# In the last stretch of a macaron block, ACT and PE take over POOL's share of the routed sum

## What is computed

```python
x = x + 0.5 * ffn(layernorm(x))       # first feed-forward
x = x + attn(layernorm(x))
x = x + 0.5 * ffn(layernorm(x))       # second feed-forward, the same weights

# ffn(h): probs = softmax(h @ gate_W.T); the two largest are the gates
routed = sum over the 2 chosen e:  gate_e * (silu(h @ w1_e) * (h @ w3_e)) @ w2_e
shared = sum over the 8 shared n:  (silu(h @ w1_s) * (h @ w3_s)) @ w2_s / 8
ffn = 0.5 * shared + 0.5 * routed
```

## Time and profile before

| | |
|---|---|
| median of 3 executions | 809.51 us (806.77 to 810.10) |
| the profiled execution | 809.17 us |
| its span, first to last instruction | 807.4 us |
| PE busy in the span | 701.7 us (87%) |
| DVE busy | 456.2 us (57%) |
| ACT busy | 347.4 us (43%) |
| POOL busy | 445.1 us (55%) |
| last routed result on its way to DRAM | 765.3 us |
| the 16 loads of YF issued | 768.15 to 780.98 us |
| mean granted TensorE clock | 0.952 of full speed |

### The profile page before, as it was taken

One profiled execution on the slowest core, in us unless ns is written; L12 is line 12 of the kernel. 1 busy time (PEld: TensorE's weight loads), 2 busy tenths in 40 slices (PEclk: granted clock), 3 DMA queues, 4 the chain that ended last, 5 costly groups with the idle time before them and its releaser, 6 DMA issues. The chain is left out here.

```text
span 807.4 us, 12924 instructions
## 1 busy us (share of the span) xinstructions
PE 701.7 (87%) x4308; PEld 596.7 (74%) x4308; DVE 456.2 (57%) x1100; ACT 347.4 (43%) x889; POOL 445.1 (55%) x511
## 2 busy tenths in 40 slices
PE   3878987999999999957876699874999999999966
PEld 3766765888888888825654487663888888888855
DVE  7598672434444444359999828763444444443375
ACT  3612642444444444477764262551444444444410
POOL 6792017566766673479886250006566667664460
PEclk9979997999999999979999989996999999999988
DMA  9700002111111120221101000001111111111182
GB/s 310 273 1 1 1 4 54 37 46 49 48 46 48 47 49 28 72 72 53 41 13 40 27 27 1 1 2 42 37 48 47 47 50 47 48 46 32 37 241 72
DMA packets 45150, 44.03 MB, mean 55 GB/s; under 512 B 6048, under 2 KB 39840, under 8 KB 44704
## 3 DMA queue, kind: packets, MB, share of 16 engines
q1 hardware_dynamic: 35872, 24.32, 9.8%
q0 software_dynamic: 9216, 18.89, 8.3%
HBM read 27.46 MB, written 15.73 MB: 53 GB/s over the span
## 5 line engine op out<-in xcount | busy, mean ns | idle before, releaser
L598 POOL DMA_INDIRECT rows<-tokens,source x144 | 139.0, 965 | 160.2 <-issue 95.9
L613 POOL DMA_INDIRECT results<-yout,target x144 | 141.7, 984 | 112.9 <-DVE yout L937 76.2
L731 DVE TENSOR_TENSOR hr<-silu,psU 128x512 f32<-128x512 f32 x144 | 99.2, 689 | 180.7 <-PE psU L1229 179.4
L1149 ACT ACTIVATE silu<-psG 128x512 f32<-128x512 f32 x144 | 86.2, 598 | 186.4 <-PE psG L1229 186.2
L1379 PE MATMUL psY<-W,hT 128*128 x1120 | 147.9, 275 | 0.0
L1379 PEld LDWEIGHTS psY<-W,hT 128*128 128x128 f32 x1120 | 136.1, 192 | 0.0
L1142 ACT ACTIVATE hT<-psH 128x512 f32<-128x512 f32 x144 | 86.0, 597 | 78.2 <-PE psH L1362 78.2
L1362 PE MATMUL psH<-ident,hr 128*128 128x128 f32 x576 | 86.5, 272 | 0.0
L1362 PEld LDWEIGHTS psH<-ident,hr 128*128 128x128 f32 x576 | 71.9, 140 | 19.0 <-issue 0.2
L1227 PE MATMUL psG<-W13H,xTH 128*128 x144 | 69.6, 484 | 3.0 <-DVE xTL L913 3.0
L1100 ACT ACTIVATE silu<-psG 128x512 f32<-128x512 f32 x64 | 37.6, 591 | 79.4 <-PE psG L1229 54.9
(11 more groups left out here) (175 smaller groups left out, 1288.5 us busy)
## 6 DMA issues: line engine op xcount, KB each, us to landing
W<-w_e SPq DMA_DIRECT2D x3, 2048.0 KB, 14.2
tokens<-XN SPq DMA_DIRECT2D x16, 256.0 KB, 2.9
Y<-results SPq DMA_DIRECT2D x32, 128.0 KB, 2.3
YF<-results SPq DMA_DIRECT2D x16, 256.0 KB, 4.9
rows<-tokens,source POOLq DMA_INDIRECT x144, 2.5
results<-yout,target POOLq DMA_INDIRECT x144, 2.3
X<-x SPq DMA_DIRECT2D x8, 256.0 KB, 5.4
out<-X SPq DMA_DIRECT2D x8, 256.0 KB, 2.5
```

What stands on the lines that cost most here:

```text
L598: pool.indirect_dma_start(rows[:, g % RING, t, :], None, tokens, bass.IndirectOffsetOnAxis(ap=source[:, tile:tile + 1], axis=0))\
L613: pool.indirect_dma_start(results, bass.IndirectOffsetOnAxis(ap=target[:, tile:tile + 1], axis=0), yout[:, g % 2, t, :], None).then_inc(y_ ...
L731: dve.tensor_tensor(hidden, silu[:, s.u % 2, :], psU[:, s.u % 2, :], ALU.mult).then_inc(h_done, 1)
L1149: act.activation(silu[:, s.u % 2, :], psG[:, s.u % 2, :], ACT.Silu).then_inc(silu_done, 1)
```

## The change

POOL no longer adds anything in the tail. Chunks 0, 2 and 4, now `PE_CHUNKS`, are done by three engines. ACT scales each half of such a chunk by its gates in place, four copies of 128x128 behind silu(25) to silu(30): chunk 0 at k = 25 and 26, chunk 2 at 27 and 28, chunk 4 at 29 and 30. PE adds the two halves of a chunk in PSUM, two fp32 matmuls of 512 columns with the identity into a bank of `last_y`, behind in_shared(28), in_shared(30) and at k = 32, ahead of out_shared(28). DVE adds the bank to X, one instruction a chunk, one step later (k = 29, 31 and 33). DVE's own five chunks stay as they are, and so does their order. SP waits for the new semaphore for chunks 0, 2 and 4.

```diff
-POOL_CHUNKS = (0, 2, 4)
-DVE_CHUNKS = tuple(c for c in range(CHUNKS) if c not in POOL_CHUNKS)
+PE_CHUNKS = (0, 2, 4)
+DVE_CHUNKS = tuple(c for c in range(CHUNKS) if c not in PE_CHUNKS)
 HALF_STEP = 24
+SCALE_STEP = 25
+SUM_STEP = {28: 0, 30: 1, 32: 2}
+SUM_LAG = 1
...
 # POOL
-            link = Chain(pool, last_link_pool)
-            pool.wait_ge(sh_added, CHUNKS + FRONT[1])
-            for c in POOL_CHUNKS:
-                pool.wait_ge(yf_in[c], 16 * TOPK)
-                chunk = slice(c * CH, (c + 1) * CH)
-                ys, xs = YF[:, :, chunk, :], X[:, chunk, :]
-                link.then(pool.tensor_tensor(ys, ys, gates[:, :, chunk].unsqueeze(3).to_broadcast([P, TOPK, CH, D]),
-                                             ALU.mult))
-                link.then(pool.tensor_tensor(xs, xs, ys[:, 0, :, :], ALU.add))
-                pool.tensor_tensor(xs, xs, ys[:, 1, :, :], ALU.add).then_inc(last_added_pool, 1)
...
 # DVE
+                    def add_sums(n):
+                        dve.wait_ge(last_summed, n + 1)
+                        chunk = slice(PE_CHUNKS[n] * CH, (PE_CHUNKS[n] + 1) * CH)
+                        xs = X[:, chunk, :].rearrange("p t d -> p (t d)")
+                        dve.tensor_tensor(xs, xs, last_y[n % 2][:, :], ALU.add).then_inc(last_added_sums, 1)
+
                     for k in range(front[1], SHARED):
                         gated_shared(Step.of(k, 2 * FT))
                         if k % FT == 6 % FT and k // FT > FRONT[1]:
                             add_shared(k // FT - 1)
                         if k >= HALF_STEP:
                             add_half()
+                        if k - SUM_LAG in SUM_STEP:
+                            add_sums(SUM_STEP[k - SUM_LAG])
                     add_half()
+                    for k in range(SHARED, SHARED + 2):
+                        if k - SUM_LAG in SUM_STEP:
+                            add_sums(SUM_STEP[k - SUM_LAG])
                     dve.wait_ge(last_link, len(DVE_CHUNKS))
                     add_shared(CHUNKS - 1)
                     add_half()
...
 # ACT
                 for k in range(front[l], SHARED):
                     silu_shared(k)
+                    if l == 1 and k >= SCALE_STEP:
+                        n, half = divmod(k - SCALE_STEP, TOPK)
+                        if n < len(PE_CHUNKS):
+                            act.wait_ge(yf_in[PE_CHUNKS[n]], 16 * TOPK)
+                            for t in range(PE_CHUNKS[n] * CH, (PE_CHUNKS[n] + 1) * CH):
+                                i = act.activation(YF[:, half, t, :], YF[:, half, t, :], ACT.Copy,
+                                                   scale=gates[:, half, t:t + 1])
+                            i.then_inc(last_scaled, 1)
...
 # PE
+                def sum_results(n):
+
+                    pe.wait_ge(last_scaled, TOPK * (n + 1))
+                    if n == 0:
+                        pe.wait_ge(y_done, 2 * GROUPS)
+                    if n >= 2:
+                        pe.wait_ge(last_added_sums, n - 1)
+                    chunk = slice(PE_CHUNKS[n] * CH, (PE_CHUNKS[n] + 1) * CH)
+                    for k in range(TOPK):
+                        i = pe.matmul(last_y[n % 2][:, :], ident[:, :],
+                                      YF[:, k, chunk, :].rearrange("p t d -> p (t d)"),
+                                      start=(k == 0), stop=(k == TOPK - 1))
+                    i.then_inc(last_summed, 1)
+
                 for k in range(front[l], SHARED + 2):
                     if k < SHARED:
                         in_shared(Step.of(k, 2 * FT))
                     if k >= front[l] + 5:
                         out_shared(Step.of(k - 5, 2 * FT))
+                    if l == 1 and k in SUM_STEP:
+                        sum_results(SUM_STEP[k])
```

More of the change, by code:

```diff
@@ L392, in macaron @@
         last_link = sem("last_link")
-        last_link_pool = sem("last_link_pool")
         last_added = sem("last_added")
-        last_added_pool = sem("last_added_pool")
+        last_scaled = sem("last_scaled")
+        last_summed = sem("last_summed")
+        last_added_sums = sem("last_added_sums")
         routed_added = sem("routed_added")
@@ L486, in _ @@
                             sp.dma_start(YF[:, k, chunk, :], results_v[:, k, chunk, :]).then_inc(yf_in[c], 16)
-                    by_pool, by_dve = 0, 0
+                    by_pe, by_dve = 0, 0
                     for c in range(CHUNKS):
-                        if c in POOL_CHUNKS:
-                            by_pool += 1
-                            sp.wait_ge(last_added_pool, by_pool)
+                        if c in PE_CHUNKS:
+                            by_pe += 1
+                            sp.wait_ge(last_added_sums, by_pe)
                         else:
```

## The result

The changed kernel takes 802.51 us in the median of 5 runs (801.18 to 803.00), the kernel before 809.51 (806.77 to 810.33, five runs): a ratio of 0.9918, 95% interval 0.9899 to 0.9938. The profiled execution took 803.0 us with a span of 801.1. The prediction was 802.8 us.

The account below looks back on a forecast made before the run. The prediction took PE, waiting for DVE that POOL slows, as what holds up the tail. Waits and low clock of 11.5 us go, 5.2 of sums and 0.1 of wait come: 809.17 - 6.4 = 802.8 us, range 800.4 to 805.6.

Parts of the forecast that it names:

- the schedule: PE and DVE carried through the tail: PE bounds it from 774.8 to 796.3, what remains starts 6.4 us earlier.
- The cause: POOL, not the loads, slows DVE's `add_half` in the tail; without it two halves take 7.1 us less.
- The slower rival: In the tail the loads, not POOL, slow DVE and sums come on top: +4.5 to 5, some 814 us; chance 0.04.
- The sums: On PE in the tail, two fp32 matmuls of 512 columns take 1.73 us a sum, 5.2 us for three.
- out(c): The shared expert's second product on PE in the tail: 3.78 us, 3.84 in the last one.
- ACT: Scaling in the tail takes 1.17 us per four copies, mostly idle time; the rival that it comes late: 804.2 us, chance 0.05.
- PE as the bound: With POOL silent, PE bounds the tail from 774.8 to 796.3, with one gap of 0.1 us.
- The rival of the cheap sums: Tail sums at 0.93 us end PE 2.4 us earlier, h(31) late by up to 1.6: some 801 us; chance 0.05.
- The output transfers: SP's queue at the end of the tail: cost taken as 0, bound 0.5 us.
- The low clock as a term: PE's half speed in the tail costs 2.4 us and goes; the rival that it still falls: 805.2 us, chance 0.09.
- The cross-check: On PE between 774.76 and 802.7, 11.5 us of waits and low clock go, 5.2 of sums and 0.1 of wait come.

Follow-up runs that it names:

- pe_4: The changed kernel with chunks 0 and 2 given to DVE, only chunk 4 left to ACT and PE: ratio 0.9886 to the kernel before, 0.9882 when repeated.
- before_pe_filler: The kernel before with useless fp32 matmuls on PE in the tail, three ahead of its wait for h(25), five ahead of h(26): ratio 1.0008.
- before_no_pool: The kernel before with POOL's nine tail instructions left out and nothing in their place: 801.6 us, ratio 0.9892.
- dve_all: The changed kernel with all eight chunks done by DVE in halves, POOL adding nothing, no part on ACT or PE: ratio 0.9878 to the kernel before.

## Why the prediction was right, and where not

With the later landing of 0.44 us taken off, the schedule held almost to the row: h(26) at 777.72 (forecast 777.72), U28 at 778.46 (778.47), the first sum added at 784.91 (784.9), in(30) at 785.85 (786.07), out(28) at 792.16 (792.4), the last `add_shared` at 796.01 (796.35).

- *The cause.* POOL's reads, not the loads and not POOL as such: shown by leaving POOL out, by bringing reads back, and by writes alone. The slower rival, sums on PE with DVE still slow, was priced at 4.5 to 5 us over before; bringing POOL's reads back makes just that case, and it took 3.8 us more than before (+0.6%).
- *The sums.* 1.73 us each was taken from two 256-column matmuls; the chain has 1.72:

```profile
779.86 1.72 PE psY L1418 x4
...
782.97 3.57 PE psH L1308 x32
```

- *out(c)* was set at 3.78 us and took 3.57 on the chain, 0.2 less. This is most of what makes the forecast tail 0.3 us too long.
- *ACT* was never late: a group of four takes 1.17 us (776.50 to 777.67), as the earlier trace rows had it.
- *PE as the bound* was right for the changed kernel, but it is a bound with little behind it: with one matmul a sum less, 2.6 us on PE, the tail gave 2.2; with no sums at all only 1.6 to 1.9 come, and even these only if something else keeps PE at work. The rival of the cheap sums let h(31) be late by up to 1.6 us; with one matmul a sum PE waited 0.18 for it.
- *The output transfers* were taken as 0 with a bound of 0.5 us. The end behind `add_shared(7)` grew by 0.04 in the changed kernel, but by 0.7 in pe_4.
- *The low clock as a term.* The cross-check took 9.1 us of waits and 2.4 us of low clock as two things that go, and in the changed kernel both went. The size of the second is borne out by before_pe_filler (1.8 us won and 0.6 waited). What the prediction had no term for is that the low clock can come back at another wait: it did so ahead of out(28) in before_no_pool and before_pe_filler, where PE got there early without sums (in dve_all it did not). The sums were a cost and a cover in one, and the forecast counted them as a cost alone.

What stays open: why the clock falls in one wait and not in another of the same length (below), and why the later chips take 75 to 81 us longer outside the tail.

## What to carry to other kernels

When DVE is slow in some stretch only, set its long instructions against POOL's in the timeline: if each ends just behind a POOL instruction and both read two tensors in SBUF, as here, work that is "spread" over both engines is done one by one, and POOL had better be silent or only write. Before giving such work to PE and ACT, count what DVE can do alone, its waits included: here it does all of it, with a tail 1.4 to 1.7 us shorter than with three chunks on PE. One chunk on PE is faster than three, and by its trace 0.9 us shorter to the end of the span than none, which the whole times don't show; the shortest trace is that of ACT scaling and DVE adding, with nothing on PE. What is removed from PE has to be priced with the clock that the new wait leaves behind.

## What was not expected of the hardware

A wait of about 2 us ahead of the same 32 matmuls brought the low clock in before_no_pool (1.88 us, then 5.46 us for the matmuls) and in before_pe_filler (1.92, 5.46), and did not in the kernel before (1.89, then 3.84) nor in dve_all (2.0 us, clock 1.00 from 870 to 876). Nothing in these traces ahead of the wait tells them apart that I could find. Nor does the fall come at one distance from the start of the wait. In before_no_pool PE went idle at 789.17 and the clock fell as PE came back at 791.05 (mean 0.84 in 790.80 to 791.20, then 0.50). In before_pe_filler PE went idle at 883.18 and came back at 885.09, and the clock fell only behind that (1.00 up to 885.60, 0.77 in 885.60 to 886.00, then 0.50). POOL's memsets of 1024 values, 953 ns each, cost DVE's two-input instructions nothing.
